# Graph attention and a mixture of experts on one core: the first batch's q/k stacks issued from SyncE in two halves

## The reference, cut to what matters

```python
def _L0_gnn_ref(x, adj_matrix, Wq, bq, ...):           # x here is the layer norm of the input
    q = (x @ Wq.T + bq).reshape(B, N, H, Dh).transpose(0, 2, 1, 3)      # k, v alike; H = 4, Dh = 32
    kc = k.reshape(B, H, Nc, CHUNK, Dh)                                  # 8 chunks of 128 keys
    scores = jnp.clip(jnp.einsum('bhnd,bhjcd->bhnjc', q, kc) / sqrt(Dh), -10.0, 10.0)
    scores = jnp.where(mask == 0, -10.0, scores)
    attn = softmax(scores, axis=-1)                                      # within each chunk
    ctx = einsum('bhnjc,bhjcd->bhnd', attn, vc)
    return layernorm(ctx @ Wo.T + bo + x) * gamma + beta
x = x + _L0_gnn_ref(_layernorm(x), adj, ...)
x = x + _L0_ffn_ref(_layernorm(x), ...)                                  # 8 experts, the best 2 of each row
```

## Time and profile before

| | us |
|---|---|
| median of 3 runs | 874.87 |
| the three runs | 874.42, 874.87, 2024.2 |
| the profiled execution's own time | 875.36 |
| its span, from the first to the last instruction | 873.6 |
| PE busy in the span | 731.4 |
| DVE busy in the span | 735.1 |
| ACT busy in the span | 579.6 |

### The profile page before, as it was taken

One profiled execution on the slowest core, in us unless ns is written; L12 is line 12 of the kernel. 1 busy time (PEld: TensorE's weight loads), 2 busy tenths in 40 slices (PEclk: granted clock), 3 DMA queues, 4 the chain that ended last, 5 costly groups with the idle time before them and its releaser, 6 DMA issues.

```text
span 873.6 us, 20979 instructions
## 1 busy us (share of the span) xinstructions
PE 731.4 (84%) x6443; PEld 375.9 (43%) x6443; DVE 735.1 (84%) x2121; ACT 579.6 (66%) x1136; POOL 555.8 (64%) x569
## 2 busy tenths in 40 slices
PE   4379699999999999999999885846313999999995
PEld 2312223323323233233232223735202888888884
DVE  4668999999999999999999999876621888878883
ACT  4367577897897978979977675535002666666662
POOL 1210547797887987978879998677771444444443
PEclk9579989999999999999999997555555999999998
DMA  8962201403204014041050003001111222222210
GB/s 284 266 93 72 74 1 36 111 2 102 46 25 122 2 43 104 2 108 38 26 121 2 1 2 97 17 22 45 53 54 42 53 56 68 67 67 63 56 48 1
DMA packets 46448, 54.40 MB, mean 62 GB/s; under 512 B 7540, under 2 KB 29137, under 8 KB 46338
## 3 DMA queue, kind: packets, MB, share of 16 engines
q10 hardware_dynamic: 13824, 25.17, 11.1%
q1 hardware_dynamic: 27554, 19.31, 8.8%
q0 software_dynamic: 4960, 8.58, 3.1%
HBM read 34.03 MB, written 20.75 MB: 63 GB/s over the span
## 4 chain that ended last, share of the span: by engine, by line
PE 43%; DVE 30%; POOL 10%; issue 9%; DMA 3%; ACT 2%; SPq 1%; POOLq 0%; ACTq 0%; DVEq 0%
DVE rspread L957 7%; PE score_ps L1438 7%; PE sum_ps L1452 6%; PE side_ps L1468 6%; DVE w L936 6%; DVE prob_ring L936 5%; POOL rows_dram L550 5%; PE sum_ps L1676 4%; PE score_ps L1398 2%; PE score_ps L1399 2%; PE score_ps L1400 2%; PE sum_ps L1678 2%; PE sum_ps L1682 2%; PE sum_ps L1680 2%; DVE prob_ring L946 2%
## 5 line engine op out<-in xcount | busy, mean ns | idle before, releaser
L1438 PE MATMUL score_ps<-stack_mem 128*128 128x512 f16 x512 | 158.1, 392 | 28.5 <-DVE prob_ring L936 13.5
L709 ACT ACTIVATE prob_ring<-prob_ring 128x1024 f32<-128x1024 f32 x128 | 134.1, 1053 | 49.7 <-DVE prob_ring L936 38.5
L936 DVE SCALAR_TENSOR_TENSOR w<-score_ps,limit 128x1024 f32<-128x1024 f32 x128 | 152.7, 1211 | 17.0 <-PE score_ps L1438 16.8
L490 POOL TENSOR_TENSOR ctx_sb<-ctx_sb,rspread 128x512 f32<-128x512 f32 x108 | 139.3, 1290 | 41.7 <-DVE rspread L957 33.4
L557 POOL DMA_INDIRECT out_x<-xn,limit x91 | 89.5, 983 | 115.8 <-DVE xn L1300 109.9
L709 ACT ACTIVATE w<-w 128x1024 f32<-128x1024 f32 x128 | 134.1, 1054 | 43.0 <-DVE w L936 42.3
L936 DVE SCALAR_TENSOR_TENSOR prob_ring<-score_ps,limit 128x1024 f32<-128x1024 f32 x128 | 153.1, 1202 | 0.9 <-PE score_ps L1438 0.7
L495 POOL TENSOR_TENSOR ctx_acc<-ctx_acc,ctx_sb 128x512 f32<-128x512 f32 x93 | 119.2, 1281 | 7.3
L831 ACT ACTIVATE xn<-score_ps,vec 128x128 f32<-128x128 f32 x364 | 103.9, 368 | 14.9 <-PE score_ps L1400 14.8
L1438 PEld LDWEIGHTS score_ps<-stack_mem 128*128 128x128 f16 x512 | 29.4, 98 | 192.9 <-issue 78.4
L957 DVE STREAM_SHUFFLE rspread<-prob_ring 128x256 f32<-128x256 f32 x256 | 101.4, 448 | 0.0
(11 more groups left out here) (227 smaller groups left out, 1488.6 us busy)
## 6 DMA issues: line engine op xcount, KB each, us to landing
stack_mem<-qk_dram ACTq DMA_DIRECT2D x64, 256.0 KB, 4.8
ctx_sb<-rows_dram SPq DMA_DIRECT2D x91, 66.5 KB, 1.9
qk_dram<-qk_hi ACTq DMA_DIRECT2D x16, 256.0 KB, 3.0
qk_dram<-qk_lo ACTq DMA_DIRECT2D x16, 256.0 KB, 3.8
x<-in_adj SPq DMA_DIRECT2D x4, 512.0 KB, 7.5
ctx_sb<-in_adj SPq DMA_DIRECT2D x4, 512.0 KB, 10.0
w<-in_L_ffn_W SPq DMA_DIRECT2D x4, 512.0 KB
rows_dram<-gather SPq DMA_DIRECT2D x29, 66.5 KB, 8.9
```

Source lines behind the costliest of these rows:

```text
L490: pool.tensor_tensor(fresh, fresh, by, ALU.mult).then_inc(scaled_ready, 1)
L709: act.activation(prob_at(s, u), prob_at(s, u), ACT.Exp, scale=1.0 / SCORE).then_inc(exp_done, 1)
L936: dve.scalar_tensor_tensor(out=prob_at(s, u), in0=score_ps[:, 2 * u:2 * u + 2, :], scalar=-LIMIT * SCORE, in1=limit[:, k:k + 1, half * HAL ...
L1438: ins = pe.matmul(score_ps[:, h, :], kstack[:, par, h, k * P:k * P + P], qstack[:, par, h, half * HALF:half * HALF + HALF], start=True, st ...
```

## The change

SP now issues batch 0's stack DMAs, behind its setup loads and a wait for all four stores. Each is cut in two by columns: 8 DMAs of 128 KB with columns 0 to 511 add to a new semaphore, `stacked_half`, and 8 more with the other columns add to `stacked`. ACT's loop over the mask has no issue in it any more. `load_x(2)` stands behind the 16 issues and waits for `stacked_half` as well; the fillings stand behind it and wait for `stacked` to be 256, which it is when the stacks of batch 1 are there. PE waits for `stacked_half` before step 0 of batch 0 and for `stacked` before step 4; for later batches its wait is as before. Batches 1 to 7 are still stacked from ACT in whole DMAs.

```diff
@@ SyncE, setup
+            sp.wait_ge(parts_stored, 64)
+            for c in range(2):
+                for i in (c, 1 - c):
+                    dst, order = stacks_of(i)
+                    for r, part in enumerate(order):
+                        sp.dma_start(dst[DH * r:DH * r + DH, 0, :, c * HALF:c * HALF + HALF],
+                                     qk_dram[2 * i + part].rearrange("(h d) n -> d h n", h=HEADS)[:, :, c * HALF:c * HALF + HALF]
+                                     ).then_inc(stacked if c else stacked_half, 16)
+
             sp.wait_ge(mask_made, T)
+            sp.wait_ge(stacked_half, 16 * STACKS)
             load_x(2)
 
             sp.wait_ge(consts_ready, CONSTS)
+            sp.wait_ge(stacked, 16 * STACKS * 2)
@@ ScalarE, setup
             for k in range(T):
-                if k == 3:
-
-                    for i in range(2):
-                        stack_parts(0, 0, i)
                 act.wait_ge(mask_turned, k + 1)
@@ TensorE, scores
-                if s == 0 and u == 0:
+                if b == 0 and s == 0 and u == 0:
+                    pe.wait_ge(stacked_half, 16 * STACKS)
+                if (s == T // 2 if b == 0 else s == 0) and u == 0:
                     pe.wait_ge(stacked, 16 * STACKS * (b + 1))
```

More of the change, by code:

```diff
@@ L254, in gnn_moe @@
         stacked = sem("stacked")
+        stacked_half = sem("stacked_half")
         v_proj_done = sem("v_proj_done")
@@ L354, in batches, with stacks_of @@
                 body(b)
+        def stacks_of(i):
+            return ((qstack, (0, 0, 1, 1)), (kstack, (0, 1, 0, 1)))[i]
         out_rows = out.rearrange("b n d -> (b n) d")
@@ L661, in stack_parts @@
             def stack_parts(bb, par, i):
-                both = isinstance(bb, int) and bb == 0
-                act.wait_ge(parts_stored, 64 * bb + (64 if both else 32 * i + 32))
-                dst, order = ((qstack, (0, 0, 1, 1)), (kstack, (0, 1, 0, 1)))[i]
+                act.wait_ge(parts_stored, 64 * bb + 32 * i + 32)
+                dst, order = stacks_of(i)
                 for r, part in enumerate(order):
```

## The result

| us | before | after |
|---|---|---|
| median | 876.64 (4 runs, 874.42 to 878.41 and one of 2024.2) | 861.62 (4 runs, 860.70 to 863.16) |
| ratio | | 0.9839, 95% interval 0.9803 to 0.9874 |
| the profiled execution's own time | 875.36 | 860.70 |
| its span | 873.6 | 858.9 |

The ratio and its interval are of the fast runs alone; the median of 876.64 still counts the run of 2024.2, without which it is 874.87. The kernel got faster by 1.6%, 11 to 17 us by the interval, within the 2% that the prediction named. Lines of the changed kernel are 11 to 16 higher than before: L1438 is now L1451, L936 is L947, L671 on ACT has its counterpart in L403 on SP.

What follows compares the result with a forecast made beforehand. The last stack DMA's landing was taken to bound batch 0's start; first scores move from 48.40 to 35.1, gaining 13.3 us, the rest hidden and the clock zero. Profiled 875.36 - 13.3 = 862.1, median 861.6; own range 860 to 863.5, to 867 with A and B.

Steps and rivals of the forecast that it cites:

- What bounded the start: Start of batch 0: last stack DMA's landing sets the first scores at 48.40; over half the traffic is not awaited.
- The landing: First half of batch 0's stacks, issued by SP from 27.4, lands at 34.2 to 35.0 us.
- The transfer's 6.8 us from batch 1: Batch 1's megabyte in four DMAs, first issue to landing, taken as the first half's time; completions may add some tenths.
- The mask: Start of batch 0: without ACT's issues, PE's 2.74 us stall goes and its last mask transposes end at 34.85.
- Rival B: Mask chain gets no faster, ACT's stall having another cause; PE starts at 37.6, gain 10.8, time 864.1 us; chance 0.05.
- The first scores: Batch 0, step 0: start at 35.1 instead of 48.40, some tenths behind the later of stacks and mask.
- What hides the rest: Second half before step 4 (cover 6 us), later x (cover 18 us) and fillings behind batch 1's stacks cost nothing.
- The clock: PE's clock rises in batch 0: sooner or later worth 1 to 2 us in all, taken as zero.
- the 13.3 of the sum: Gain in us from first scores moving from 48.40 to 35.1, with the whole loop moving forward by that much.
- Rival A: Stack halves: small DMAs dearer than their bytes, half lands at 39.2 to 40, time about 866 us; chance 0.12.
- Rival C: PE's clock stays low in PE-bound steps, 2.9 us more each; eight steps cost 23 us, time 885; chance 0.02.
- Rival D: First half: DMA fixed part paid eight times in a row, landing at 46.8, gain 1.6, time 873.3 us; chance 0.01.

Runs made afterwards that it cites:

- The first experiment: Kernel before, with one more wait on SP holding x of batches 4 to 7 and the fillings until the first batch's stacks landed; 870.15 us, ratio 0.9932.
- the kernel with the spread alone: Changed kernel with DVE's inverse root for batches 4 to 7 spread, one part each, over steps 14, 15 and batch 1's 0 to 3; 862.12 us.
- the kernel with x first: Changed kernel with x of batches 4 to 7 issued ahead of the stack halves on SP's queue; 869.87 us, ratio 0.9928.
- without SP's waits: Changed kernel without SP's waits for stacked_half before x and for the second batch's stacks before the fillings; 862.01 us, ratio 0.9842.

## Why the prediction was right

**What bounded the start** was read rightly: the landing of the stacks, with more than half of the traffic not needed. The first experiment shows the second part alone: 6.2 us by one more wait, which held x and the fillings back.

**The landing.** Predicted 34.2 to 35.0, measured 35.25. The stores landed at 27.29 (said 27.4), the issues took 0.47 us each (0.46). The transfer's 6.8 us from batch 1 were too few: 7.3 alone, 7.95 with the second half behind it. The last is an omission, since I let the second half start for nothing. This is the term that was mis-sized: 1.15 us above the 6.8, of which the tenths added for four more completions, 0.8 at most, covered the greater part.

**The mask** was to end at 34.85 and ended at 33.93. Taking out ACT's stall was worth its 2.74 us, the rest is PE's clock: in the changed kernel's repeat and in the kernel with the spread alone, where the clock stood at 0.50 through the mask as before, the last transposes ended at 34.99 and 34.69, in both 8.40 us behind the start of the first, against 37.59 - 26.32 = 11.27 before. Rival B is thus refuted.

**The first scores** at 35.30 against 35.1, gain 13.1 against 13.3, and 35.51 in the repeat. DVE's slack was said to be 0.7 us and was 0.48.

**What hides the rest** held in all three points: no wait at step 4, x read at 67.98 (said 68.2) 21 us after it had landed, the fillings from 85.10 (said 85.3) with no engine waiting for them.

**The clock** was put at zero, with 1 to 2 us in the range. The change got 0.4 us from it, at the first clip: it came 0.74 us behind the first scores, where the prediction had kept the 1.2 us of before. The other microsecond, by which the span fell by 14.7 and not 13.5 between the first two profiles, is scatter: the repeat's span fell by 13.5, close to the 13.3 of the sum. That the median came out at 861.62 against 861.6 is luck in part: the first three runs before had a median of 874.87, 17 others 876.12, and the changed kernel's repeat gave 864.02. With sets that differ by 1 to 2 us for the same kernel, an agreement to 0.02 us is chance.

**Rival A** (small DMAs) is refuted for this size: at most 0.5 us on 2.1 MB, and 7.3 us for a megabyte in eight DMAs against 6.8 in four. **Rival C** did not occur; in every profile the clock was back at the high level by 60 us. **Rival D**, with eight fixed parts one after another, had wanted the half at 46.8 and fails by the same numbers.

**One to one.** Over the twelve profiles the first clip lies between 35.4 and 49.6 us and the stretch from the first to the last clip between 471.6 and 474.7, with no trend (472.7 at 49.6, 474.7 at 43.3, 473.7 at 35.6). What is won ahead of the loop is kept, to within the 3 us of scatter in the loop, of which only the parts named above are traced to the clock.

## What to carry to other kernels

When an engine waits for a load, list everything that the DMA engines move in that stretch and ask of each piece when it is first read; holding back what is needed later can be worth as much as making the needed load smaller or sooner. Split a load where the first consumer needs only a part, and leave everything that can wait behind it on the same queue: the order of the queue suffices without further waits. And before a gain of a microsecond is credited to a change, look at where PE's granted clock rose in each of the compared executions, and profile the same kernel a second time: here that took the microsecond away again.

## What the runs showed of the hardware that was not expected

- SP's DMA issue is not always 0.35 to 0.47 us. Behind the x load of 4096 rows of 512 B the next issue took 5.43 us in the kernel with x first, and the profile before had shown it already: the first filling, right behind x, took 5.66 us there (5.53 with the competing loads held back, 6.49 without SP's waits) and 0.36 in the changed kernel with an empty queue. The 29 fillings took 23.97 us before, with stacks and x in flight, 20.23 behind x with the stacks landed, and 14.07 in the changed kernel, alone.
- A megabyte queued behind slows the one ahead at its end: the first half landed 7.9 to 8.0 us after its first issue in the five profiles with the second half right behind it, 7.3 and 7.2 in the two without.
- The clock of PE rises and falls at other times from one execution to the next although the program is the same. In two executions of the changed kernel it fell ahead of the mask transposes and rose again at 29.4 in one and at 35.0 in the other, and behind the pause at 101.1 and 103.3. The Trainium skill's page "TensorE: Matmul & The Clock Gate" (Part 1) calls the point of the rise variable from run to run; the trace agrees. Here it makes 1.0 us in the stretch behind the pause (4.63 to 5.62), and 1 us more ahead of it: 62.6 to 62.9 us from the first clip to the scores behind the pause in the four profiles in which the clock rose 10.5 to 11.1 us behind the first scores, 61.5 to 61.8 in the six that have the same work and an earlier rise.
- In the profile with x first, DVE's last four pieces of the mask took 5.28 us instead of 2.49, which made the mask late by 2.5 us; the cause was not tested.
